# V's diagonal blocks written by ScalarE from PSUM in four copies, in an attention and GRU kernel

## The reference, cut to what matters

```python
xn = _rms_norm(x, g_norm) * (1.0 + scale) + shift
q, k, v = split_heads(xn @ W_qkv)              # 16 heads of 16
q, k = _rms_norm(q, g_q), _rms_norm(k, g_k)
attn = softmax(einsum('bhqd,bhkd->bhqk', q, k) * d ** -0.5)
o = einsum('bhqk,bhkd->bhqd', attn, v)
x = x + o + o @ W_out
x = x + gru_scan(cond, x)                      # 32 steps over the tokens
```

## Time and profile before

| | us |
|---|---|
| median of 3 runs | 365.77 (365.37 to 367.87) |
| the profiled execution | 367.55 |
| its span in the profile | 365.4 |

### The profile page before, as it was taken

The page is one execution under the profiler, slowest core; times in us unless marked ns, Lnnn a source line. Parts: engine busy times, 40 slices in busy tenths (PEclk is TensorE's granted clock), DMA queues, the critical chain, the costliest instruction groups (busy, mean ns, idle before and its releaser), DMA issues.

```text
span 365.4 us, 12913 instructions
## 1 busy us (share of the span) xinstructions
PE 340.2 (93%) x4305; PEld 304.0 (83%) x4305; DVE 263.0 (72%) x667; ACT 226.4 (62%) x668; POOL 205.5 (56%) x383
## 2 busy tenths in 40 slices
PE   8588899999999999999779999999999999999990
PEld 7466778878877887887567999999999999999990
DVE  2568999999999999999877355555555555555554
ACT  4567877787778778776543655555555555555442
POOL 5477777777777777777522433444444444444330
PEclk9899999999999999999999999999999999999997
DMA  6993322323222222222220011111111111111112
GB/s 201 340 315 86 90 76 70 90 79 84 80 65 78 80 77 66 80 80 71 75 67 4 2 25 29 27 29 26 28 29 26 27 26 27 26 27 29 29 28 32
DMA packets 54767, 24.90 MB, mean 68 GB/s; under 512 B 40770, under 2 KB 49620, under 8 KB 54740
## 3 DMA queue, kind: packets, MB, share of 16 engines
q1 hardware_dynamic: 54036, 23.73, 25.9%
q10 hardware_dynamic: 704, 0.82, 0.6%
HBM read 7.48 MB, written 4.19 MB: 32 GB/s over the span
## 4 chain that ended last, share of the span: by engine, by line
PE 72%; SPq 11%; DMA 6%; DVE 4%; issue 3%; ACT 1%; POOL 1%; DVEq 0%; POOLq 0%; ACTq 0%
PE bank L1041 33%; PE bank L1093 24%; SPq L391 6%; SPq L383 6%; PE bank L1187 4%; PE bank L1168 4%; PE bank L1156 3%; DMA operands<-operands 2%; PE bank L1148 2%; DMA v_diag<-v_rows 2%; DMA x_in<-in_x_dram 1%; PE bank L1139 1%; PE bank L1106 1%; PE bank L1047 1%; POOL operands L447 1%
## 5 line engine op out<-in xcount | busy, mean ns | idle before, releaser
L1093 PE MATMUL bank<-h,w_hh_sb 128*128 128x128 f32 x768 | 95.0, 278 | 0.2
L1093 PEld LDWEIGHTS bank<-h,w_hh_sb 128*128 128x128 f32 x768 | 90.7, 191 | 2.0 <-issue 0.5
L1013 DVE SCALAR_TENSOR_TENSOR operands<-bank,vec_cols,operands 128x128 f32<-128x128 f32 x64 | 22.2, 347 | 47.1 <-ACT operands L754 47.1
L1041 PE MATMUL bank<-pair_hi,wih_hi 128*128 128x256 f32 x180 | 52.7, 293 | 0.0
L754 ACT ACTIVATE operands<-bank,bsum 128x128 f32<-128x128 f32 x64 | 22.9, 358 | 46.4 <-PE bank L1093 45.2
L553 POOL TENSOR_TENSOR operands<-operands,h 128x128 f32<-128x128 f32 x64 | 29.5, 461 | 38.5 <-ACT operands L755 38.5
L1041 PE MATMUL bank<-pair_lo,wih_hi 128*128 128x256 f32 x180 | 50.4, 280 | 0.0
L1041 PE MATMUL bank<-pair_hi,wih_lo 128*128 128x256 f32 x180 | 50.3, 279 | 0.0
L1041 PE MATMUL bank<-wqkv_hi,xn_hi 128*128 128x256 f32 (+1 forms) x128 | 48.7, 380 | 0.9 <-ACT v_rows L635 0.5
L562 POOL TENSOR_TENSOR operands<-h,x2T 128x256 f32<-128x256 f32 x31 | 22.5, 725 | 46.8 <-issue 34.1
L1041 PE MATMUL bank<-wqkv_lo,xn_hi 128*128 128x256 f32 (+1 forms) x128 | 43.6, 341 | 0.0
(11 more groups left out here) (120 smaller groups left out, 856.2 us busy)
## 6 DMA issues: line engine op xcount, KB each, us to landing
v_diag<-v_rows SPq DMA_DIRECT2D x128, 34.0 KB, 1.9
operands<-operands SPq DMA_DIRECT2D x64, 64.0 KB, 2.0
operands<-operands SPq DMA_DIRECT2D x32, 128.0 KB, 2.0
out_dram<-operands SPq DMA_DIRECT2D x254, 16.0 KB, 1.4
x_in<-in_x_dram SPq DMA_DIRECT2D x7, 512.0 KB, 9.6
w_hh_sb<-in_L_cond_W_hh_dram SPq DMA_DIRECT2D x1, 768.0 KB, 8.8
stage_w<-in_L_cond_W_ih_dram SPq DMA_DIRECT2D x1, 768.0 KB, 10.6
w_emb_sb<-in_L_cond_W_emb_dram ACTq DMA_DIRECT2D x1, 512.0 KB, 4.6
```

Of the source, the lines that this page charges most:

```text
L1013: dve.scalar_tensor_tensor(out=rh[:, c, :], in0=xnh[:, HN_COL:HN_COL + B], scalar=bhh[:, 2 * KC + c:2 * KC + c + 1], in1=r_g[:, c, :], op0 ...
L1041: last = pe.matmul(dst, a, w, start=start and i == 0, stop=i == len(terms) - 1, skip_group_check=True)
L1093: last = pe.matmul(dst, gate(w_hh_sb, name, c)[k], moving, start=k == 0 and (name == "n" or opens and name == "z"), stop=k == KC - 1, skip ...
```

## The change

ScalarE writes V's four blocks itself: `values` makes four copies of 32 rows each from `p_v` into `v_diag`, and the last one raises `v_ready`. The tile `v_rows`, SP's four transfers a group and their two semaphores are gone. PE's attention product waits for `v_ready`. The ones are set once in `v_diag` by four small memsets on POOL.

```diff
-SP_V, SP_KEYS = 5, 6
+SP_KEYS = 6
-        v_rows = sb("v_rows", [P, 2, HEADS, VW])
-        v_diag_ready = [sem("v_diag_ready0"), sem("v_diag_ready1")]
-            sp.wait_ge(ones_ready, 2)
-            def place_values(v, slot, place):
-                sp.wait_ge(v_ready, v + 1)
-                for b in range(GB):
-                    rows = slice(T * b, T * b + T)
-                    sp.dma_start(v_diag[rows, place, b, :, :].rearrange("p h f -> p (h f)"),
-                                 v_rows[rows, slot, :, :].rearrange("p h f -> p (h f)"))\
-                      .then_inc(v_diag_ready[slot], 16)
...
-            pool.memset(v_rows[:, :, :, DH:VW], 1.0).then_inc(ones_ready, 1)
             pool.memset(v_diag[:, :, :, :, :], 0.0).then_inc(ones_ready, 1)
+            pool.wait_ge(ones_ready, 1)
+            for b in range(GB):
+                pool.memset(v_diag[T * b:T * b + T, :, b, :, DH:VW], 1.0).then_inc(ones_ready, 1)
...
-            def values(v, slot):
+            def values(v, place):
                 act.wait_ge(v_ps, v + 1)
+                if isinstance(v, int) and v == 0:
+                    act.wait_ge(ones_ready, 1 + GB)
                 if later(v, 4):
                     act.wait_ge(o_ps, v - 3)
-                if later(v, 2):
-                    act.wait_ge(v_diag_ready[slot], spread(v - 2, slot, GB))
-                act.copy(v_rows[:, slot, :, 0:DH], p_v.rearrange("p (h d) -> p h d", h=HEADS)).then_inc(v_ready, 1)
+                for b in range(GB):
+                    rows = slice(T * b, T * b + T)
+                    last = act.copy(v_diag[rows, place, b, :, 0:DH], p_v[rows, :].rearrange("p (h d) -> p h d", h=HEADS))
+                last.then_inc(v_ready, 1)
...
             def attention_products(g, slot, place):
                 pe.wait_ge(probsT_ready, g + 1)
-                pe.wait_ge(v_diag_ready[slot], spread(g, slot, GB))
+                pe.wait_ge(v_ready, g + 1)
```

More of the change, by code:

```diff
@@ L395, in body @@
             def body(base, u):
-                v = group(base, u, SP_V)
-                if v is not None:
-                    place_values(v, (u - SP_V) % 2, (u - SP_V) % 4)
                 g = group(base, u, SP_KEYS)
@@ L401, in body @@
                     place_keys(g, (u - SP_KEYS) % 2)
-            pipeline(sp, body, NG - 1 + max(SP_V, SP_KEYS))
+            pipeline(sp, body, NG - 1 + SP_KEYS)
             out_blocks = out.rearrange("(j q) t (c i a) -> i q c j t a", q=PB, c=KC, a=PB)
@@ L510, in _ @@
             pool.memset(threes[:, :], 3.0).then_inc(threes_ready, 1)
-            pool.memset(v_rows[:, :, :, DH:VW], 1.0).then_inc(ones_ready, 1)
             pool.memset(v_diag[:, :, :, :, :], 0.0).then_inc(ones_ready, 1)
+            pool.wait_ge(ones_ready, 1)
+            for b in range(GB):
+                pool.memset(v_diag[T * b:T * b + T, :, b, :, DH:VW], 1.0).then_inc(ones_ready, 1)
             pool.wait_ge(threes_ready, 1)
-            pool.wait_ge(ones_ready, 2)
+            pool.wait_ge(ones_ready, 1 + GB)
             first = [norm_first[:, i, 0:FIRST_PAIR] for i in range(7)]
@@ L700, in body @@
                 if v is not None:
-                    values(v, (u - ACT_V) % 2)
+                    values(v, (u - ACT_V) % 4)
                 d = group(base, u, ACT_X2T)
```

## The result

The changed kernel takes 387.3 us (median of 4 runs, 386.55 to 387.7); the kernel before, on the same chip, 366.7 (365.37 to 367.87). The ratio is 1.056 (95% interval 1.051 to 1.061). Slower by 5.6%, where I forecast no change (366.8, range 358.0 to 371.5), and slower than my dearest rival (376.9). The profiled span grew by 19.2 us, from 365.4 to 384.6.

A forecast was written before the change was run, and what follows sets the result against it. A cycle between GpSimd and VectorE, 5.30 us a turn, was taken to set the loop's pace. Fill -0.6, loop +4.7 and end -3.1 gave +1.0 on 365.77: 366.8 us, range 358.0 to 371.5.

The forecast's parts named there:

- my dearest rival: ScalarE's V copies spend the whole 0.35 each: turn 5.96, loop +11.9, sum +11.1, 376.9 us; chance 0.18.
- The loop's chain: Loop, turns 12 to 32: oT_lo starts 0.30 later, `ms4` stays held by xn_lo, 5.60 a turn against 5.30, +4.7 us.
- The copy's price: ScalarE's V copies: 0.26 each, upper bound 0.35; the three extra cost 0.78 us a turn.
- The fill: Pipeline fill: V's wait of 1.94 goes, extra copies of turns 4 to 6 cost 2.34, partly hidden; net -0.6 us.
- My 4.89 a turn: Fill, turns 7 to 12: the next bound, ScalarE to VectorE and back; five turns 24.4 against 24.3, so even.
- What I had put at no price: Side edits: `v_ready` 0.78 later, ScalarE's queue behind its longer step, POOL's four memsets; no further cost.
- The three turns after the loop: The three turns between the loop and the end: called even, bound +1.1 us.
- The end: End of stage: the last three scores' waits, 3.35 us, come from keys' transfers behind V's on SP; -3.1 us.
- No V copy is left in the drain: End of stage: no V copies remain there, so they add nothing to it.
- the fourth rival: End of stage: the keys' six last transfers land late by themselves, the 3.1 don't come, 369.9 us; chance 0.09.
- The absorbing rival: Loop: ScalarE's 1.13 us idle takes in the 0.78, turn stays 5.30, sum -5.0, 360.8 us; chance 0.08.

The follow-up runs named there:

- The kernel whose copies really stand 0.26 apart: The changed kernel with all four copies reading and writing rows 0 to 31, so V is wrong for three of four sequences: 371.6 us, ratio 1.015.

## Why the prediction was wrong, point by point

**The loop's chain: right.** The forecast walked from the end of `ms4` over ScalarE to oT_hi, oT_lo, xn_lo and back, and had 5.60 a turn at 0.26 a copy. The kernel whose copies really stand 0.26 apart has 5.60. With the measured 1.51 for the four in place of 1.04 the same sum gives 5.60 + 0.47 = 6.07; measured 121.91 / 20 = 6.10. `ms4` stayed held by xn_lo in the loop (0.68 and 0.76 in the rows above), as taken.

**The copy's price: the step that failed.** "Its length per partition is the same 256 columns, so I take 0.26 each." It was 0.38. This single term is most of the miss: 0.47 x 20 = 9.4 us in the loop, of the 9.9 by which it missed, and the kernel with the price I had taken measures 371.6, 15.7 less than the changed one. My reasoning compared sizes. But the 0.26 in the rows was the distance between instructions that all start at partition 0, and the overlap that it shows (0.35 long, 0.26 apart) is lost when the first partition moves. In the kernel before every instruction of ScalarE's turn starts at partition 0, so no row could show such a move. I named this as the ground of the rival ("no row has four copies with disjoint partitions of one tile") and gave it 0.18; its bound of 0.35 was itself low, since a held copy takes 0.37 and the next one begins 0.01 later.

The Trainium skill has the mechanism, on the page "VectorE: DVE Perf Modes", section "Two Vector instructions with no wait between them", as a model for VectorE alone: an instruction whose input or output starts in another quadrant than the last one's starts only when all earlier ones have finished. The runs here agree with it for ScalarE in each of four cases: both sides moving (1.51), the output alone (1.49), the input alone (1.51), neither (1.04).

The rule of the Trainium skill that I did weigh ("VectorE: DVE Perf Modes", section "The TRN2 errata — SBUF-src ops pay a fixed extra latency per instruction"), 172 cycles and the columns per copy, gave an estimate of 1.43 us for the four and 5.99 a turn. That is nearer to the measured 1.51 than my row, but not for its reason: four copies of 128 rows that stay put take 1.04.

**The fill: missed, -0.6 against +2.9.** V's wait of 1.94 did go, and SP's queue did cease to bound turns 7 to 12: between 32 and 56 us the chain of waits before is SP's queue for 95%, and after it has none of it. That alone could gain little, since the next bound lay close below (4.77 a turn without transfers or extra copies, against 4.87 before). That the copies would then set the pace was right, too. My 4.89 a turn with 0.47 more gives 5.36; measured (58.25 - 32.04) / 5 = 5.24. So it is the same term again. With copies 0.26 apart the fill came out at +0.1. What I had put at no price, `v_ready` rising later, gave TensorE six waits of 0.28 to 0.40 us in the fill and none in the loop; from 32 us on the chain of waits doesn't pass them.

**The three turns after the loop: missed, 0 against +1.9.** I called them even without working them out. They too pay the copies in the chain; at 0.26 the price was +0.5.

**The end: missed, -3.1 against -0.4.** I put all three waits of TensorE down to V's transfers ahead of the keys', and took them back whole. For the first two that was so, at least in part: the masked keys were ready at 175.97 and 180.42, and their transfers were issued at 176.97 and 182.73, 1.0 and 2.3 us late, behind V's four. For the third it was not, as the chain of waits of the kernel before shows:

```profile
184.29 1.03 POOL operands L447
185.32 0.02 issue
185.34 0.51 SPq L391
...
186.52 3.72 DMA operands<-operands
190.24 0.14 issue
190.37 0.74 PE bank L1168 x32
```

SP issued these at once, and the last of them landed 3.72 us after its issue. After the change the first two waits are gone, 2.2 us, and the third is 1.21 where it was 1.11.

The copies then took most of the 2.2 back: "No V copy is left in the drain" was wrong: turn 35 has V's last copies, and x2T, qkT and so the masked keys stand behind them. The timeline after shows it: the logarithm of turn 35 at 196.94, the masked keys at 199.78, 2.84 later; before it was 177.62 to 179.38, 1.76. Without any extra copy, the end came out 2.4 us shorter.

```profile
197.34 1.48 ACT L625 COPY v_diag<-bank 32x256 f32<-32x256 f32 x4
198.84 0.37 ACT L630 COPY x2T<-bank 128x256 f32<-128x256 f32 x1
199.11 0.59 ACT L638 COPY qkT<-bank 128x512 f32<-128x512 f32 x1
199.36 0.55 PE L1139 MATMUL bank<-ident,x 128*128 128x128 f32 x2 [1.81 <-ACT x2T L630]
199.78 1.04 POOL L433 TENSOR_TENSOR operands<-qkT,gqk_parity 128x512 f32<-128x512 f32 x1 [1.03 <-ACT qkT L638]
199.84 1.10 PE L1159 MATMUL bank<-operands,qkT 64*32 64x128 f32 x32
...
209.26 0.67 PE L1159 MATMUL bank<-operands,qkT 64*32 64x128 f32 x32 [1.21 <-DMA operands<-operands]
```

TensorE stands 1.81 us for ScalarE's x2T, and then its scores take 1.10 instead of 0.67. The busy times by stretch show the granted clock there:

```profile
196.00:200.00 4.00, 2.19 (x40) 1.62 (x36) 3.26 (x9) 2.97 (x9) 1.59 (x6) 0.94 0.23 66
200.00:204.00 4.00, 3.89 (x75) 3.07 (x69) 3.19 (x7) 1.64 (x5) 1.68 (x3) 0.64 0.24 72
204.00:208.00 4.00, 4.00 (x86) 3.30 (x86) 3.86 (x10) 3.19 (x6) 1.56 (x2) 1.00 0.24 67
```

0.64 is a mix of the full level (2.4 GHz) and the half (1.2 GHz), after a stretch in which TensorE was busy for 2.19 of 4 us. It costs some of the gain (0.43 on the scores alone). In the run without extra copies the clock was 1.00 there. As an estimate from these numbers, -2.2 + 0.1 + 1.1 + 0.4 = -0.6, against the measured -0.4.

The third wait is what the fourth rival was about, that the last keys land late by themselves: the chain of waits after has the last of them landing after 3.04 us, with no transfer of V in the kernel at all.

```profile
206.09 3.04 DMA operands<-operands
209.12 0.14 issue
209.26 0.74 PE bank L1159 x32
```

With the four copies in one quadrant it took 3.88, and the last scores waited 1.07; with one copy and the very same transfers they didn't wait at all. Why the last ones take 3 to 4 us in some runs and 2.0 in others stays open; no run tests it.

**The chances.** Dear copies was the case, with 0.18, and its 376.9 was 10.4 short. Of these, 8.1 are in the stretches of the table: the loop took 2.7 more than its 11.9, the end gave back 2.7 less, the fill and the three turns took 4.8 where the rival had 2.3, and the start and the GRU 0.3 more. The median of the kernel before is 0.9 higher in the second set of runs, and the medians lie 1.4 further apart than the two profiled spans. The absorbing rival failed as I had argued: 1.13 us idle were of no use at the place where they stood, and once the copies were moved to them the loop paid nothing for the four.

## What to carry to other kernels

Idle time of an engine is a place, not a budget: find which step ends it and put added work ahead of that step; with the same four copies the kernel was 20.6 us slower than before when they stood at the head of the turn, and not measurably slower when they stood at its end. When a change splits one instruction by partitions, take for each piece the full duration, not the distance to the next instruction, unless a row shows the overlap across quadrants.

## What the runs showed of the hardware

ScalarE overlaps a copy with the next instruction when both start at the same partition (0.26 us apart for 256 columns out of PSUM, 0.36 to 0.38 long in the mean), for 32 rows as for 128. When the first partition of the input or of the output moves to another quadrant, the next starts after the end (0.38 apart), and so does the instruction that moves back: four such steps a turn, (1.51 - 1.04) / 4 = 0.12 us each. Only moves by whole quadrants were tried.

A VectorE operation of 33 columns (`ms4`) took 0.18 us when it started before GpSimd's xn_lo (104.09 and 104.17, copies last), and 0.76 when it started 0.01 after it (106.27 and 106.26, the changed kernel), ending 0.04 behind it. With it held the loop takes 5.32 to 5.37 us a turn in the kernels with one copy; with it ahead, in the one with the copies last, 5.20.
